# Cross attention's sums go to the projection's rows in SBUF, and six of eight projections move from the feed-forward into the cross stage

## The reference

```python
x = x + self_attention(layernorm(x))                        # causal
x = x + cross_attention(layernorm(x), ctx, ctx, mask)       # ctx: (4, 77, 256)
x = x + feed_forward(layernorm(x))                          # 256 -> 768 -> 256, silu(gate) * up
# inside cross_attention
scores = where(masked, -1e9, q @ k.T / 4)
out = softmax(scores) @ v          # per head
return out @ Wo                    # all heads, 256 -> 256
```

## Time and profile before

| | us |
|---|---|
| median of 3 runs | 1110.01 |
| lowest, highest | 1108.73, 1130.41 |
| profiled execution, its own time | 1113.3 |
| its span, first to last instruction | 1111.4 |

### The profile page before, as it was taken

How to read it: one execution, slowest core, us unless ns; L and a number is a source line. 1 busy time by engine, 2 the same in 40 slices (tenths; PEclk the granted TensorE clock), 3 DMA queues, 4 the chain that set the end, 5 groups by cost and what they waited for, 6 DMA issues and landing times.

```text
span 1111.4 us, 18977 instructions
## 1 busy us (share of the span) xinstructions
PE 1044.5 (94%) x7092; PEld 616.6 (55%) x7092; DVE 741.8 (67%) x1603; ACT 562.3 (51%) x1061; POOL 222.1 (20%) x199
## 2 busy tenths in 40 slices
PE   2879989999999999999999999899998899999997
PEld 2767534444444444444444466444443688888886
DVE  5999787778778778777787366555544555555552
ACT  1445236676667667667666568377655211111110
POOL 6554550000000000000000023211102233344431
PEclk9998779999999999999999899699968899999999
DMA  8259821343444444333320046687961211111101
GB/s 249 96 202 231 261 46 26 71 69 71 78 79 81 83 79 79 81 66 69 67 49 15 5 96 167 151 201 177 217 153 54 71 50 46 50 48 48 46 20 38
DMA packets 85458, 105.26 MB, mean 95 GB/s; under 512 B 12542, under 2 KB 73642, under 8 KB 83831
## 3 DMA queue, kind: packets, MB, share of 16 engines
q1 hardware_dynamic: 82871, 100.89, 38.3%
q10 hardware_dynamic: 2496, 3.16, 1.4%
HBM read 61.80 MB, written 37.06 MB: 89 GB/s over the span
## 4 chain that ended last, share of the span: by engine, by line
PE 72%; DVE 19%; DMA 3%; ACT 2%; issue 2%; SPq 1%; POOL 1%; POOLq 0%; DVEq 0%; ACTq 0%
PE bank L135 18%; PE bank L838 11%; PE bank L807 10%; PE bank L824 9%; DVE pm L736 8%; PE bank L1097 3%; PE bank L1450 2%; PE bank L828 2%; PE bank L1335 2%; PE bank L1337 2%; PE bank L937 2%; PE bank L1345 2%; PE bank L812 2%; PE bank L1320 2%; PE bank L1322 2%
## 5 line engine op out<-in xcount | busy, mean ns | idle before, releaser
L736 DVE TENSOR_REDUCE pm<-bank 128x1 f32<-128x512 f32 (+3 forms) x608 | 356.8, 654 | 87.7 <-PE bank L812 71.2
L784 ACT ACTIVATE prob<-bank 128x512 f32<-128x512 f32 (+1 forms) x608 | 317.6, 584 | 186.3 <-PE bank L828 99.3
L807 PE MATMUL bank<-stk,stq 96*128 96x512 bf16 (+3 forms) x768 | 227.5, 340 | 4.7 <-DVE pm L736 2.5
L824 PE MATMUL bank<-stq,stk 98*128 98x512 bf16 (+3 forms) x768 | 222.6, 330 | 0.7 <-ACT prob L784 0.5
L838 PE MATMUL bank<-prob,va 128*17 128x512 f32 (+3 forms) x1536 | 145.5, 497 | 0.0
L807 PEld LDWEIGHTS bank<-stk,stq 96*128 96x128 bf16 x768 | 68.8, 98 | 136.9 <-DVE pm L736 81.0
L1545 ACT ACTIVATE e_sg<-bank 128x512 f32<-128x512 f32 x48 | 28.7, 598 | 187.9 <-PE bank L135 187.9
L957 POOL TENSOR_TENSOR c_rstd<-c_ve,mhalf 128x4 f32<-128x4 f32 x8 | 8.1, 1009 | 498.0 <-DVE c_ve L128 498.0
L1297 ACT ACTIVATE xprob<-bank 80x512 f32<-80x512 f32 x128 | 72.4, 591 | 65.9 <-PE bank L1337 64.6
L824 PEld LDWEIGHTS bank<-stq,stk 98*128 98x128 bf16 x768 | 69.5, 99 | 45.0 <-ACT prob L784 9.3
L812 PE MATMUL bank<-tri_q,identb 128*128 128x128 bf16 (+2 forms) x352 | 88.4, 251 | 0.0
(11 more groups left out here) (172 smaller groups left out, 1399.9 us busy)
## 6 DMA issues: line engine op xcount, KB each, us to landing
qk<-a_parts SPq DMA_DIRECT2D x32, 384.0 KB, 4.3
od<-xu SPq DMA_DIRECT2D x16, 512.0 KB, 4.6
xq<-c_parts SPq DMA_DIRECT2D x16, 384.0 KB, 3.1
xstq<-xq SPq DMA_DIRECT2D x32, 192.0 KB, 4.7
stq<-qk SPq DMA_DIRECT2D x30, 192.0 KB, 4.0
stk<-qk SPq DMA_DIRECT2D x15, 384.0 KB, 6.3
vs<-a_vst SPq DMA_DIRECT2D x8, 544.0 KB, 4.7
oall<-u_out SPq DMA_DIRECT2D x64, 64.0 KB
```

The lines of the kernel that those rows point to most:

```text
L736: nc.vector.tensor_reduce(pm[:, k, h0:h0 + hb, r], src[:, 0:hb * w].rearrange("p (h w) -> p h w", h=hb), AX, ALU.max).then_inc(s_mxe, 1)
L784: nc.scalar.activation(prob[:, U % NPS, 0:hb * n], bank[STB[U % NSB]][:, 0:hb * n], ACT.Exp).then_inc(s_ex, 1)
L807: mm = nc.tensor.matmul(dst[:, h * w:(h + 1) * w], stq[i][0:R, half, h0 + h, r * P:(r + 1) * P], stk[i][0:R, h0 + h, k0:k0 + w], start=(h ...
L824: mm = nc.tensor.matmul(dst[:, h * n:(h + 1) * n], stk[i][0:RM, h0 + h, kt * P:(kt + 1) * P], stq[i][0:RM, half, h0 + h, q0:q0 + n], start ...
```

## The change

The sums no longer go through DRAM. `store_sums3` copies the four heads of a group from `xu` straight into the projection's rows `oall2` in SBUF (four DMAs of 16 rows) and the softmax's sums into `den2` (a fifth). `vx` keeps one column of ones instead of 16. `shares3` inverts and splits on VectorE at the end of the group with i = 1; SP stores the shares at the end of its own loop turn for that group and loads them back in the middle of the next one, behind `load_cross` and a row of maxima. The items `s` (spread, one for each half of the 256 columns) and `o` (projection, two a chunk) then stand in TensorE's maxima ring, in the groups with i = 2 and 3, and take the same three banks; VectorE multiplies after an `s` and adds to x after an `o`. So chunks 0 to 5 are projected in the cross stage; 6 and 7 in the feed-forward, in the loop turns c = 1 and 2 (`LATE_AT`). POOL's quotients, `load_ffn`, and the DRAM tensors `od2` and `rdn2` are gone. The weights are loaded in groups 0, 3 and 7 instead of 0, 1 and 6. The moments of chunk 0 are taken at the end of group 13, its normalising after group 14.

```diff
+        def cross_items(g):
+            todo = [[] for u in range(NST2)]
+            b, i = g // GB - 1, g % GB
+            if b >= 0 and i == 2:
+                todo[4].append(("s", 2 * b, 0))
+                todo[5].append(("s", 2 * b, 1))
+                todo[7].append(("o", 2 * b, 0))
+            if b >= 0 and i == 3:
+                todo[0].append(("o", 2 * b, 1))
+                todo[1].append(("s", 2 * b + 1, 0))
+                todo[2].append(("s", 2 * b + 1, 1))
+                todo[4].append(("o", 2 * b + 1, 0))
+                todo[6].append(("o", 2 * b + 1, 1))
+            if g + AHEAD - 1 < G:
+                todo[LATE2].append(("t", g + AHEAD - 1, 1))
+            if g + AHEAD < G:
+                ring = maxima_of(g + AHEAD)
+                for n, item in enumerate(ring):
+                    todo[LATE2 + n * (NST2 - LATE2) // len(ring)].append(item)
+            return todo
...
                 if g + 1 < G:
                     maxima(g + 1, 1)
+                if b >= 0 and i == 2:
+                    load_shares3(sp, b)
                 if g:
-                    store(g - 1)
+                    store_sums3(sp, g - 1)
                 if g + AHEAD < G:
                     maxima(g + AHEAD, 0)
...
-                b = g // GB - 1
-                if b >= 0 and g % GB == 1:
-                    for w in range(2):
-                        sp.wait_ge(xus[w], 16 * 2 * (b + 1))
-                    load_den2(sp, b)
-                if b >= 0 and g % GB == 2:
-                    store_inverse(sp, b)
-                if 7 <= g < 7 + 2 * KT:
-                    load_ffn(sp, (g - 7) // KT, [(g - 7) % KT])
-            store(G - 1)
+                if g in (0, 3, 7):
+                    load_weight(sp, (0, 3, 7).index(g))
+                if b >= 0 and i == 1:
+                    store_shares3(sp, b)
+            store_sums3(sp, G - 1)
...
-            for c in range(2):
-                quotients3(g, c)
...
+                elif kind == "s":
+                    o = sums_of(g, m)
+                    nc.vector.tensor_tensor(o, src[:], o, ALU.mult).then_inc(xs_mxe, 1)
+                elif kind == "o":
+                    x_ = xres[:, g, 2 * m:2 * m + 2].rearrange("p j d -> p (j d)")
+                    nc.vector.tensor_tensor(x_, src[:], x_, ALU.add).then_inc(xs_mxe, 1)
...
+                if kind == "s":
+                    t.wait_ge(s_rl2, 16 * (g // 2 + 1))
+                    nc.tensor.matmul(dst[:], sel[:, m], shares_of(g), start=True, stop=True).then_inc(xs_mxf, 1)
+                    return
+                if kind == "o":
+                    t.wait_ge(xs_mxe, place2["s", g, KT - 1] + 1)
+                    project3(dst, g, m).then_inc(xs_mxf, 1)
+                    return
...
+        def store_sums3(sp, g):
+            b, i = g // GB, g % GB
...
+            sp.wait_ge(xs_u, 2 * g + 2)
+            for h in range(HG):
+                row = HD * (HG * (i % 2) + h)
+                sp.dma_start(oall2[row:row + HD, b % 2, i // 2],
+                             xu[h * VW:h * VW + HD, g % 2]).then_inc(xus[g % 2], 16)
+            rows = S // DT * HG
+            sp.dma_start(den2[rows * i:rows * (i + 1), b % 2],
+                         xu[HD:P:VW, g % 2].rearrange("a (c t) -> a c t", t=DT)).then_inc(xus[g % 2], 16)
+
+        def store_shares3(sp, b):
+            sp.wait_ge(s_rd2, 5 * (b + 1))
+            sp.dma_start(xrd3[b].rearrange("c h (k t) -> (h k) c t", t=DT), xr3[:, b % 2]).then_inc(s_rs2, 16)
+
+        def load_shares3(sp, b):
+            sp.wait_ge(s_rs2, 16 * (b + 1))
+            sp.dma_start(rd2[:, b % 2], xrd3[b].rearrange("c h s -> (c h) s")).then_inc(s_rl2, 16)
+
+        def shares3(v, b):
+            for w in range(2):
+                v.wait_ge(xus[w], NOUT * 2 * (b + 1))
...
+            nc.vector.reciprocal(den2[:, q], den2[:, q]).then_inc(s_rd2, 1)
...
             hidden(0, 0)
             hidden(0, 1)
+            shares3(v, B - 1)
             for c in range(NCH):
                 more = c + 1 < NCH
+                if c in LATE_AT:
+                    quotients3(c - 1)
                 if more:
-                    sums3(v, c + 1)
+                    moments3(v, c + 1)
```

More of the change, by code:

```diff
@@ L1244, in cross_gpsimd, with item @@
                 ffn_weight_low(g, x)
[L1245 to L1246 removed]
             power3(g, 0)
         def cross_vector(v, first):
[L1250 to L1252 removed]
+            def item(N):
+                kind, g, m = order2[N]
                 src = bank[MXB[N % NMB]]
@@ L1268, in cross_vector @@
             if first:
-                for n in range(AHEAD * NMX2 - 1):
-                    item(n // NMX2, n % NMX2)
+                for N in range(len(lead2)):
+                    item(N)
                 return
+            N = len(lead2)
             for g in range(G):
[L1273 to L1282, removed]
+                for due in steps2[g]:
+                    for _ in due:
+                        item(N)
+                        N += 1
+                b, i = g // GB - 1, g % GB
+                if b >= 0 and i == 1:
+                    shares3(v, b)
+                if g == G - 3:
+                    moments3(v, 0)
+                if g == G - 2:
+                    normalise3(v, 0)
@@ L1352, in cross_tensor @@
                 t.wait_ge(xs_set, 32)
-                for n in range(AHEAD * NMX2 - 1):
-                    maxima(n // NMX2, n % NMX2)
+                for N in range(len(lead2)):
+                    item(N)
                 return
+            N = len(lead2)
             for g in range(G):
                 for what, which, ahead in plan2:
-                    if g == G - 1 and what == "s" and which == NST2 - 3:
-                        t.wait_ge(xs_mxe, G * NMX2)
-                        project3(t, 0)
                     if what == "s":
@@ L1365, in cross_tensor @@
                         products(g + ahead, which)
-                    elif what == "r" and g + ahead < G:
-                        maxima(g + ahead, which)
+                    elif what == "r":
+                        for _ in steps2[g][which]:
+                            item(N)
+                            N += 1
             for half in range(2):
@@ L1408, in load_ffn @@
[L1408 to L1416, removed]
@@ new lines, in sums_of, with shares_of, project3 @@
+        def sums_of(c, k):
+            return oall2[:, c // 2 % 2, k, c % 2 * CH:(c % 2 + 1) * CH]
+        def shares_of(c):
+            return rd2[:, c // 2 % 2, c % 2 * CH:(c % 2 + 1) * CH]
+        def project3(dst, c, w):
+            for i in range(2):
+                for k in range(KT):
+                    mm = nc.tensor.matmul(dst[:, i * D:(i + 1) * D], sums_of(c, k)[:, (2 * w + i) * P:(2 * w + i + 1) * P],
+                                          xwo[:, k], start=(k == 0), stop=(k == KT - 1))
+            return mm
@@ L1596, in ffn_tensor @@
                 more = c + 1 < NCH
-                if more:
-                    project3(t, c + 1)
-                for h in range(2, HT - 1):
+                if c in LATE_AT:
+                    spread3(c - 1)
+                gate_up(c, 2)
+                if c in LATE_AT:
+                    t.wait_ge(es_on, KT * c)
+                    for w in range(2):
+                        t.wait_ge(es_yo, 2 * (c - 1) + w + 1)
+                        project3(bank[OB[w]], N_LATE + c - 1, w).then_inc(es_op, 1)
+                for h in range(3, HT - 1):
                     gate_up(c, h)
```

171 lines of the change are left out of this document (85 added, 86 removed).

## The result

The changed kernel takes 1129.92 us (median of 4 runs, 1126.56 to 1135.02) beside 1109.37 for the kernel before: ratio **1.0201, 95% interval 1.0158 to 1.0244**. It is slower, by about 2%, where the forecast said 1.2%; whether by more than 2% the interval leaves open. The ratio leaves out one slow execution of the kernel before (1130.41), which the median takes in.

What follows compares the result with a forecast made beforehand. TensorE was taken to bound both the cross stage and the feed-forward. Terms -17.1 + 18.3 (stalls) + 12 (clock) = +13.2 us took the median from 1110.0 to 1123 us, 1.2% slower; range 1092 to 1140.

Steps and rivals of the forecast that it cites:

- The new wait: TensorE stands at the spread for the shares in groups 6, 10 and 14: 6.6, 6.6 and 5.1 us, sum 18.3.
- T: Start of the first score of a cross-stage group with i = 2, from which the forecast counted its steps.
- The queue: Shares' load behind the queries in ring order lands at T + 11; without that at T + 9.2, 5 us less over three stalls.
- The sum without them: All terms except the new stalls and the clock behind them: -16.4 + 19.9 - 11.2 - 8.0 - 2.9 + 1.5 = -17.1 us.
- the two stalls taken out of the kernel before: Cross-stage stands of TensorE, 1.66 and 4.00 us, with half clock behind them; their removal was priced at 11.2 and 8.0 us.
- uncovered wait at c = 0: At the feed-forward's start the last batch row's shares delay the moments; cost between 0 and 2.2 us, taken as 1.5.
- From the last product to the first gate_up: The gap before the feed-forward was to shrink from 4.8 to 2.6 us, -2.9 us with half clock counted.
- That rival: SP's store issues make queries late, so TensorE waits about 1 us in 6 to 12 groups: 1131 us, chance 0.05.
- the clock behind the stalls: Half clock after each of the three new stands costs 8/2 = 4.0 us, 12 in all, bounds 7.5 to 28.5.
- the stall at 836: In the kernel before, TensorE's 4.00 us cross-stage stand during POOL's quotients, followed by 8.00 us at half clock.
- The rival with the clock: Same three stalls, but each followed by 19 us at half clock, +16.5 us in all: 1140 us, chance 0.25.
- the one at 804: In the kernel before, TensorE's 1.66 us stand during VectorE's wait for sums from DRAM, then 19.00 us at half clock.

Runs made afterwards that it cites:

- experiment 2: The changed kernel with all eight spread and projection items of a batch row in the group with i = 3; 1097.62 us, ratio 0.9853 to the kernel before.
- kernel 6: The kernel before with VectorE's inversion one group later and the two quotients on VectorE, no projection moved; 1096.60 us, ratio 0.9872.
- Experiment 8: The changed kernel with the first projection item behind each stall one group later, the others behind it, stalls as they are; 1137.07 us, ratio 1.0237.
- 4 to 6: The kernel before with the inversion one group later (1100.86 us), with POOL's quotients on VectorE (1106.26 us), and with both (1096.60 us).
- experiment 3: The changed kernel with shares made after score step 3 of the group with i = 1, stored earlier and loaded first; 1100.96 us, ratio 0.9894.
- experiment 10: The changed kernel with twelve useless products on TensorE just before each wait for the shares; 1121.64 us, ratio 1.0105.
- experiment 4: The kernel before with VectorE's inversion, its store and the projection's loads one group later; 1100.86 us, ratio 0.9917.
- experiments 9: The changed kernel with spread and projection items later, plus six useless products in TensorE's two waits opening the cross stage; 1095.85 us, ratio 0.9860.
- experiment 11: The changed kernel with useless products before the waits for the shares, seventeen in groups 6 and 10, twelve in the third; 1120.93 us, ratio 1.0083.
- experiment 5: The kernel before with the cross stage's two quotients on VectorE, behind group 14, instead of on POOL; 1106.26 us, ratio 0.9946.

## Why the prediction was right, and where it was short

- **The new wait** held in every step: shares made by T + 3.2 (3.4 forecast), load issued T + 7.2 (7.4), landed T + 10.9 (11.0), TensorE at the spread T + 4.3 (4.4); stands of 6.74, 7.06 and 5.00 us for 6.6, 6.6 and 5.1.
- **The queue.** Landing behind the queries was one of two ends, T + 11 and T + 9.2. It took 3.70 and 4.04 us from issue, 2.13 without queries. The rule of the Trainium skill named there (DMA: Bandwidth & Descriptors, Queues, rings and completion order) agrees in direction. In experiment 1, where the load goes out ahead of the queries, it took 2.08, 2.38 and 2.95 us. But that moves the issue as well as the place in the ring, so that no run has ring order alone.
- **What the waits hide.** The sum without them was -17.1; experiment 2 measures -16.3 by the medians, about 10 either way. By the stages of its profile, with an opening stretch as long as before's, it is 1.2 more in the cross stage and 13.0 less in the feed-forward, -11.8, so that the sum may be some 5 us too good. Of its terms, the two stalls taken out of the kernel before gave 9.2 and 6.0 for 11.2 and 8.0, inside the noise, and 14.2 together for 19.2, which is not: together they were priced 5 us too high. The feed-forward shrank by 13.1 us (14 to 16 forecast), with 1.6 of uncovered wait at c = 0 (1.5). From the last product to the first gate_up it was 898.24 - 895.64 = 2.60 us (2.6). The cross stage grew by 31.9 (28 to 33). An undisturbed group took 738.64 - 730.66 = 7.98 us from product to product, against 8.07.
- **SP** kept up: no wait of TensorE for queries over 0.6 us. That rival fell.
- **The mis-sized term is the clock behind the stalls**, forecast at 3 x 4.0 = 12.0, half of 8.0 us each. The profile has (11.3 + 11.4 + 8.5) / 2 = 15.6, so it was 3.6 too low. (The 3.5 us at half clock at the feed-forward's start cost 1.7, where the forecast had counted the full clock; experiment 2, which has none of the three stands, has such a stretch too, from 869.5 to 873.) Its model was the stall at 836 in the kernel before, where the clock returned without a projection; here it returned with the first projection, which starts 7.9, 7.9 and 5.7 us behind the spread. That 8.0 us came so near to 11.3, 11.4 and 8.5 is therefore partly luck. The forecast named the projections three steps behind the spread, but only as a reason against the longer stretch, and did not count the distance, which stands in the written order.
- **The median.** From experiment 2 to the changed kernel the profile shows 18.8 of stands and 15.6 of clock, 34.4 us, where the forecast had 30.3. By the stages it is 200.3 - 169.6 = 30.7 in the cross stage and nothing in the feed-forward; the opening stretch at half clock was 10.5 us in the profile of after and 17 in those of before and experiment 2, worth 3.2, and with it the stage gives 33.9. By the medians it is 1.0201 - 0.9853 = 3.48%, 38.6 us, about 11 either way. So the change cost -16.3 + 34.4 = 18.1 us, against 20.6 between the medians and 18.8 by the stages, 22.0 with equal opening stretches. The 13.3 of the two profiled executions is smaller by the 5.4 that lie ahead of the cross stage, which the change doesn't touch: that it equals the forecast's 13.2 is luck. Why executions of one kernel differ by such stretches stays open.
- **The rival with the clock** lost here, 1140 forecast, because the projections stand close behind the spread. Experiment 8 shows that the stage's own work can leave the clock down that long: with the projections further off, 20.2, 17.6 and 15.7 us at half clock, and 1137.07. That it always does was wrong: 7.0 us in kernel 6, 3.5 in experiment 1.

The loss, then, is the place of the spreads and projections in an order, not the moved work: experiment 2 is faster than both kernels, and 4 to 6 show that the kernel before had as much to win, as far as can be told, by mending its own two stalls.

## What to carry to other kernels

Work that goes out to DRAM and back needs its whole way counted in the program order of every engine that it passes, the issuing queue's other issues too; an in-order TensorE should meet it a group later, not as soon as the plan allows. Price a stall with what follows it: here the distance to the next projection, read from the order, was a better price than the length of another stall, though the clock also came back without one. And where a change removes old stalls along with its main step, mend them by themselves in the old kernel first: here that alone brought as much as the change without its waits. Before two profiles are subtracted, compare the stages that the change leaves alone.

## What the runs showed of the hardware

- A short stand can be enough: 1.66 us, 1.86 in experiment 3 and 1.94 in experiment 10 were followed by 19, 20.5 and 6.5 us at 1.2 GHz. It need not be: one of 2.14 us in experiment 4 lies within the 108 us at 2.4 GHz above.

```profile
813.30 0.32 PE L1320 MATMUL bank<-xstk,xstq 96*128 96x80 bf16 x4 [2.14 <-DMA xstq<-xq]
```

Length of stand and length of stretch don't go together: 5.00 us had 8.5 behind it, and of two stands of 1.66 us the one at 804 had 19, the one in kernel 6 had 7.0. What decides between them is not shown.
- In all twelve half-clock stretches of the cross stage in which a projection stood (three each of after and of the experiments 1 and 8, one of 3, two of 10) the clock rose within the projection's first 128x128 block of eight products or within half a microsecond of its end, though TensorE had been busy with the stage's other products before, in experiment 3 without a gap for 16.5 us (804.5 to the projection at 820.98). They aren't the only way back: the 8 us at 839.5, the 7.0 us in kernel 6 and 3.5 us in experiment 1 ended without one. Which property of these products brings the clock back, their density, f32 or eight in a row, is not shown.
- Useless products in the gap kept the clock at 2.4 GHz (experiments 9 and 11), and where the time is lost anyway that is a gain: 1.2% from the changed kernel to experiment 11, about 0.5 either way.
- POOL's products of two SBUF tiles slowed small operations on VectorE: a 16-element cast took 2.19 us, and the subtraction behind it, 0.17 at 799.10, took 2.26:

```profile
837.09 2.26 DVE L1266 TENSOR_TENSOR xmt<-xpm,xmt 128x16 bf16<-128x16 f32 x1
```

With the products on VectorE (experiment 5) they take 0.18 and 0.17. By the Trainium skill (SBUF — State Buffer, SBUF: two separate sides) these two engines share a pair of ports that one of them locks for a whole instruction, when VectorE has two SBUF inputs or is in a mode that uses the shared pair. The trace agrees in size: each of the two took about as long as one of POOL's two products, 4.64 / 2 = 2.32.
